# First product: four output tiles share one narrow run of the low weight halves instead of two

## The reference

```python
def first(x, weight, ids):                  # x: (8, 256, 1024)
    return jnp.einsum('bsi,boi->bso', x, weight[ids])     # one 1024x1024 matrix per sequence

def ffn(xc):                                # xc = first(...), as (2048, 1024)
    probs = softmax(xc @ W_router.T)        # top 2 of 8, renormalised -> combine
    h = jnp.einsum('nd,erd->ner', xc, A_stack) * combine[..., None]
    return xc @ W_base.T + b_base + jnp.einsum('ner,eor->no', h, B_stack) * 2.0

out = x + ffn(first(x, L0_cond_weight, itok_B_3_7))
```

## Time and profile before

| | |
|---|---|
| median of three runs | 394.69 us |
| the profiled execution's own time | 394.37 us |
| its span, first to last instruction | 392.6 us |
| TensorE busy (2185 matmuls) | 388.7 us |
| VectorE busy | 302.0 us |
| ScalarE busy | 183.6 us |
| 512 wide matmuls of the first product, L828 | 123.3 us |
| 512 narrow matmuls of the first product, L832 | 66.7 us |

### The profile page before, as it was taken

The page is one execution under the profiler, slowest core; times in us unless marked ns, Lnnn a source line. Parts: engine busy times, 40 slices in busy tenths (PEclk is TensorE's granted clock), DMA queues, the critical chain, the costliest instruction groups (busy, mean ns, idle before and its releaser), DMA issues.

```text
span 392.6 us, 5707 instructions
## 1 busy us (share of the span) xinstructions
PE 388.7 (99%) x2185; PEld 332.8 (85%) x2185; DVE 302.0 (77%) x431; ACT 183.6 (47%) x281; POOL 50.0 (13%) x84
## 2 busy tenths in 40 slices
PE   8999999999999999999999999999999999999997
PEld 8888888888888888888888888888888888888886
DVE  4897966789699999974458786778867989998322
ACT  5877734758632444232147666357656224441000
POOL 0101103110002130021130000260000202201110
PEclk9999999999999999999999999999999999999999
DMA  7997875869333145586668767489083302552222
GB/s 263 391 361 281 291 269 125 283 224 334 119 107 27 56 157 169 179 279 206 215 222 275 229 230 251 117 246 387 29 264 117 72 5 81 182 167 80 82 80 80
DMA packets 21979, 73.95 MB, mean 188 GB/s; under 512 B 3344, under 2 KB 3600, under 8 KB 21952
## 3 DMA queue, kind: packets, MB, share of 16 engines
q1 hardware_dynamic: 15984, 55.58, 41.5%
q0 software_dynamic: 5680, 16.96, 14.3%
q10 hardware_dynamic: 288, 1.05, 0.7%
HBM read 64.13 MB, written 8.39 MB: 185 GB/s over the span
## 4 chain that ended last, share of the span: by engine, by line
PE 99%; DVE 0%; issue 0%
PE bank_x L828 30%; PE bank_x L832 16%; PE bank_y L813 9%; PE bank_y L815 9%; PE bank_y L814 8%; PE bank_x L815 8%; PE bank_x L814 8%; PE bank_x L813 8%; PE bank_y L883 2%; PE bank_y L959 2%; DVE out_sb L612 0%; DVE h_hl L549 0%
## 5 line engine op out<-in xcount | busy, mean ns | idle before, releaser
L828 PE MATMUL bank_x<-x_hl,wc_hl 128*128 128x512 f32 x512 | 123.3, 391 | 0.0
L553 DVE TENSOR_TENSOR wc_hl<-raw,wc_hl 128x1024 fp32r<-128x1024 f32 x90 | 108.4, 1220 | 18.5 <-ACT wc_hl L492 18.3
L492 ACT CAST wc_hl<-raw 128x1024 fp32r<-128x1024 f32 x90 | 93.6, 1051 | 56.1 <-DVE raw L557 22.9
L828 PEld LDWEIGHTS bank_x<-x_hl,wc_hl 128*128 128x128 f32 x512 | 94.1, 189 | 18.0
L832 PEld LDWEIGHTS bank_x<-x_hl,wc_hl 128*128 128x128 f32 x512 | 65.9, 191 | 2.6
L832 PE MATMUL bank_x<-x_hl,wc_hl 128*128 128x256 f32 x512 | 66.7, 283 | 0.0
L521 ACT COPY xc_low<-bank_x 128x256 f32<-128x256 f32 x64 | 23.7, 370 | 33.7 <-PE bank_x L832 21.9
L706 DVE TENSOR_TENSOR xp<-bank_x,xc_low 128x256 f32<-128x256 f32 x64 | 26.9, 421 | 15.2 <-ACT xc_low L521 14.1
L814 PE MATMUL bank_x<-x_hl,wc_hl 128*128 128x512 f32 x96 | 37.4, 389 | 0.0
L815 PE MATMUL bank_x<-x_hl,wc_hl 128*128 128x512 f32 x96 | 37.4, 389 | 0.0
L813 PE MATMUL bank_x<-x_hl,wc_hl 128*128 128x512 f32 x96 | 37.4, 389 | 0.0
(11 more groups left out here) (88 smaller groups left out, 505.5 us busy)
## 6 DMA issues: line engine op xcount, KB each, us to landing
raw<-w_cond SPq DMA_DIRECT2D x62, 512.0 KB, 4.7
raw<-w_base SPq DMA_DIRECT2D x24, 512.0 KB, 5.2
out_sb<-x POOLq DMA_DIRECT2D x32, 256.0 KB, 4.7
raw<-x SPq DMA_DIRECT2D x14, 512.0 KB, 4.8
out<-out_sb POOLq DMA_DIRECT2D x28, 256.0 KB, 2.3
raw<-x ACTq DMA_DIRECT2D x2, 512.0 KB, 3.7
raw<-w_cond SPq DMA_DIRECT2D x4, 256.0 KB, 3.5
gate_rows<-compared POOLq DMA_DIRECT2D x16, 64.0 KB, 3.9
```

Source lines behind the costliest of these rows:

```text
L492: nc.scalar.copy(split_dst(key, HI), split_src(key)).then_inc(hi_done, 1)
L553: nc.vector.tensor_tensor(split_dst(key, LO), split_src(key), split_dst(key, HI).bitcast(F32), ALU.subtract).then_inc(lo_done, 1)
L828: return nc.tensor.matmul(ps[:], wc_hl[:, slot_of(s, t), HI, k], x_hl[:, s % 2, k].rearrange("p h n -> p (h n)"), start=(k == 0), stop=stop)
```

## The change

`quad(s, t)` makes four tiles with one narrow run: 8 wide of t and of t + 1, 1 wide of t + 2 and of t + 3, then the 8 narrow of each of the four, then 7 wide of t + 2 and 7 of t + 3. It replaces two calls of `cond`. Sequence 0 keeps `first_cond` and `cond(0, 2)` and has one quad, the other sequences have two. The waits on TensorE stand ahead of the same matmuls as before. Nothing else is changed; the lists of ACT, DVE, SyncE and GpSimd are the same.

```diff
--- before.py
+++ after.py
@@ -846,13 +846,32 @@
                     if b == KT:
                         mm.then_inc(cond_done, 1)
 
-            def cond(s, t):
-
-                u = t + 1
-                pe.wait_ge(hi_done, SPLIT["w", s, t])
+            def quad(s, t):
+
+                tiles, ps = range(t, t + 4), {}
                 if t == 0:
                     pe.wait_ge(lo_done, SPLIT["x", s, 0])
                     pe.wait_ge(lo_done, SPLIT["x", s, 1])
+                for u in tiles:
+                    pe.wait_ge(hi_done, SPLIT["w", s, u])
+                    ps[u] = cond_bank(s, u)
+                    for k in range(KT if u < t + 2 else 1):
+                        wide(ps[u], s, u, k)
+                for u in tiles:
+                    pe.wait_ge(lo_done, SPLIT["w", s, u])
+                    for k in range(KT):
+                        mm = narrow(ps[u], s, u, k, stop=(u < t + 2 and k == KT - 1))
+                    if u < t + 2:
+                        mm.then_inc(cond_done, 1)
+                for u in tiles[2:]:
+                    for k in range(1, KT):
+                        mm = wide(ps[u], s, u, k, stop=(k == KT - 1))
+                    mm.then_inc(cond_done, 1)
+
+            def cond(s, t):
+
+                u = t + 1
+                pe.wait_ge(hi_done, SPLIT["w", s, t])
                 ps = cond_bank(s, t)
                 for k in range(KT):
                     wide(ps, s, t, k)
@@ -960,11 +979,12 @@
 
             for g in range(GROUPS):
                 for s in range(GSEQS * g, GSEQS * (g + 1)):
-                    for t in range(0, KT, 2):
-                        if s == 0 and t == 0:
-                            first_cond()
-                        else:
-                            cond(s, t)
+                    if s == 0:
+                        first_cond()
+                        cond(s, 2)
+                    else:
+                        quad(s, 0)
+                    quad(s, 4)
                     if s % 2:
                         router(s // 2)
                         lora_down(s // 2)
```

More of the change, by code:

```diff
@@ L847, in first_cond @@
                         mm.then_inc(cond_done, 1)
+            def quad(s, t):
+                tiles, ps = range(t, t + 4), {}
+                if t == 0:
+                    pe.wait_ge(lo_done, SPLIT["x", s, 0])
+                    pe.wait_ge(lo_done, SPLIT["x", s, 1])
+                for u in tiles:
[13 more added lines that the diff above has]
+                    mm.then_inc(cond_done, 1)
             def cond(s, t):
@@ L852, in cond @@
                 pe.wait_ge(hi_done, SPLIT["w", s, t])
-                if t == 0:
-                    pe.wait_ge(lo_done, SPLIT["x", s, 0])
-                    pe.wait_ge(lo_done, SPLIT["x", s, 1])
                 ps = cond_bank(s, t)
```

## The result

The changed kernel takes 407.32 us, the median of 6 runs (406.28 to 408.43), against 394.71 for the kernel before in the same session: ratio 1.0319, interval 1.0309 to 1.0329. The forecast was 405.3 with a range to 408.5. The profiled execution takes 406.53 us.

The account below looks back on a forecast made before the run. TensorE, busy 99% of the span, was taken as the bound; stalls of 10.9 us less 0.3 for changes of width gave +10.6 on 394.37, 405.0, with the median 0.32 higher 405.3 us; range 401.5 to 408.5.

Parts of the forecast that it names:

- What bounds it, and the due time: First product: TensorE busy 99% and never waiting; quads ask for the fourth weight tile's high half 3.5 us earlier.
- Q + 15.02: Q is a quad's start; the next quad's fourth weight tile is due at Q + 11.13 + 3.89.
- all six waits: Sequence 0 into 1 +2.15, inside 2 +1.46, 2 into 3 +3.47, 4 into 5 +1.02, inside 6 +1.46, 6 into 7 +1.02 us.
- The correction for sequence 2 into 3: Tile 4 is finished later, so its copy and x cast end later than DVE took that split: +0.49 us with the handover.
- Changes of width: TensorE, sequences 0 to 7: 15 fewer alternations of wide and narrow runs at 0.02 us, -0.3 us; ends 0 and -0.45.
- the sign that the prediction named: TensorE in the profile after: narrow runs of 32, wide runs of 32, and no longer pitch behind them.
- Ends of odd sequences: Router in sequences 1 and 5 waits for DVE's sum of tile 7, 0.15 us each, +0.3 us.
- the hand-over: From the end of a cast to the matmul that waits for it: taken as 0.2 us, from the kernel's start.
- The clock: TensorE's granted clock: the +10.6 us sum has no term for a fall; the forecast as it stands got 65%.
- Rival C: TensorE's clock falls in a stall, 2.6 us each: 407.9 after the 3.5 us stall alone; chance 13%.
- the case of 410.5: Clock falls after the 3.5 us stall and the 2.15 one too, total 410.5 us; left outside the range.
- Loads and GpSimd: Raw-slot loads and GpSimd's residual loads, put at nothing: split some 11 us later against 4.7 us to landing.

Follow-up runs that it names:

- run 1: Changed kernel with the weight splits of steps 6 and 7 ahead of the cast and subtraction of xc in even sequences; 398.10 us, ratio 1.0086.
- run 6: Changed kernel with splits of steps 6 and 7 ahead in even sequences and gating at steps 2 and 3 of sequences 3 and 7; 396.16 us.
- run 2: Changed kernel with the gating of h done at steps 2 and 3 of sequences 3 and 7 instead of 2 and 6; 404.15 us, ratio 1.0237.

## Why the prediction was right

*What bounds it, and the due time.* Right: the rule that the fourth weight tile is due at Q + 15.02, with the time of the cast's end read from the old rows and shifted to the new end of its tile, gave the length of all six waits within 0.03 us. The correction for sequence 2 into 3 was needed: without its 0.49 the wait would have been put at 2.98 and not 3.47. In the trace after, that cast starts at 91.60 and the waiting matmul follows:

```profile
91.60 1.04 ACT L492 CAST wc_hl<-raw 128x1024 fp32r<-128x1024 f32 x1
```

91.60 + 1.04 = 92.64 and the bracketed matmul starts at 92.69, 0.05 us later; with its slower successor (0.11) that makes the 0.16 for which I had taken 0.2.

*Changes of width.* Right: 0.019 us each. The formula of the Trainium skill ("TensorE: Matmul & The Clock Gate", section "Back-to-back issue gap"), which gives the gap of isolated matmuls from the columns alone, is not enough here: matmuls of 512 columns are spaced 0.2267 us in a row of their own kind and more for the first six behind a narrow run (0.233, 0.237, 0.228, 0.232, 0.230, 0.228 by their starts from 39.95 on). The measurement decides, though it is worth only 0.3 us. The slower pitch behind a narrow run is still there, against the sign that the prediction named; there are only fewer such places.

*Ends of odd sequences.* Wrong by 0.3 us: there is no wait in front of the router. The sum of tile 7 ended at 55.80 and its consumer, the last eighth of a router that starts at 54.36 and takes 1.88 us, comes at about 56.0. The working had it 0.15 short, mostly because it took 0.2 for the hand-over, where the one just measured took 0.05; a margin of that size is beyond such rows.

*The clock.* The forecast put the clock at nothing, and this is the step that failed: the belief that a wait of 2 to 3.5 us leaves the clock alone most of the time. Rival C was given 13% and was in fact every case: all six executions had at least one fall and four had two, so the median lies 2 us above the forecast. That it still lies inside the range owes something to luck, since the same rival had the price of a fall too high: 2.6 us from the start of the kernel, 1.5 measured here. With the true number of falls and that price it would have been the case of 410.5, outside the range. In the opening stretch of the kernel before, 24 of the 25 distances are 0.21 us; behind a fall only 16 of the 32 narrow ones are, at 0.213 instead of 0.12. The profile gives a granted clock of 1.00 for that opening, so that it ran at the 1.2 GHz level was read from the pitch alone; the same pitch of 0.213 under a reading of 0.51 supports it. The Trainium skill's rule (same page, "HAM oscillation — how this bites in real kernels"), that a TensorE which waits between bursts drops to half rate, is borne out at the waits of 3.45 us (in 3 of 3 profiles) and of 2.12 us (in 2 of 4). Behind the waits of 1.97 us or less between quads no profile shows a fall. But the fall at the start in run 1 came behind brackets of 0.89 and 0.68 us, while 1.89 us in one piece at the start of run 6 had none, so the length of the wait does not decide alone.

*Loads and GpSimd.* Put at nothing, and rightly for the quads: all six waits of TensorE are ended by ACT, none by a DMA. Only the start of the kernel depends on loads, as before.

## What to carry to other kernels

When a reordering saves issue cost on the bounding engine, first write down two times for every buffer it touches: when it is now asked for and when its predecessor is now finished. If helpers serve their lists in order, the time from a tile's end to its successor's readiness can be read off the old trace and shifted, which gave each wait here to 0.03 us. Moving work out of the way helps only if it lands where there is slack; one step later, two thirds of it returned. And a wait of some 2 us on TensorE should be priced above its length, because the clock can fall behind it: here by 1.5 us a fall.

## What the hardware showed that was not expected

The clock fell behind a wait of only 2.12 us, and not each time: in the profiled execution of the changed kernel it stayed up there and fell behind the wait of 3.45; with that one filled it fell at 2.12; in the profile of run 2 at both. What TensorE had done before was the same at these places, 31 wide matmuls in a row and then the wait. Each fall stretched the narrow run behind by 1.4 to 1.5 us. By the granted clock of the executions the times order themselves: no fall in the five with both waits filled (404.35 to 405.43), one at 406.28 and 406.53, two at 407.26 to 408.43. The sums for these are 404.9, 406.4 and 407.9 us. What decides whether the clock falls behind a wait of 2.12 us stays open, and so does what made it fall at the start in run 1.
